# A gated attention stage with a shorter tile pipeline, GpSimd taking the scale and the add into X for six of eight groups, and another order of loads

## Time and profile before

| what | value |
|---|---|
| median of 3 runs | 2098.03 us |
| the 3 runs | 2091.5, 2098.03, 2098.66 us |
| the profiled execution | 2095.7 us, span 2093.8 us |
| PE busy over the span | 1423.5 us (68%) |
| DVE busy over the span | 1382.9 us (66%) |
| ACT busy over the span | 1120.2 us (54%) |
| POOL busy over the span | 498.2 us (24%) |

### The profile page before, as it was taken

The page is one execution under the profiler, slowest core; times in us unless marked ns, Lnnn a source line. Parts: engine busy times, 40 slices in busy tenths (PEclk is TensorE's granted clock), DMA queues, the critical chain, the costliest instruction groups (busy, mean ns, idle before and its releaser), DMA issues. The chain is left out here.

```text
span 2093.8 us, 33634 instructions
## 1 busy us (share of the span) xinstructions
PE 1423.5 (68%) x11186; PEld 871.1 (42%) x11186; DVE 1382.9 (66%) x2946; ACT 1120.2 (54%) x1552; POOL 498.2 (24%) x903
## 2 busy tenths in 40 slices
PE   3339999999569965988616666368998836675111
PEld 3315555555357742444411333235555522443010
DVE  6647878878244533587667999435565557874896
ACT  4517777777411213665527889523343426886454
POOL 4412233333310032111013343100101011211663
PEclk9999999999879986999855667679999958887555
DMA  5653555555310002333110000011101030000111
GB/s 168 203 123 76 127 128 128 134 127 133 69 46 0 0 5 40 67 66 67 37 64 1 0 1 0 26 31 27 36 24 37 12 106 1 1 1 9 42 50 41
DMA packets 100486, 118.01 MB, mean 56 GB/s; under 512 B 33825, under 2 KB 86249, under 8 KB 95757
## 3 DMA queue, kind: packets, MB, share of 16 engines
q1 hardware_dynamic: 100364, 116.48, 22.1%
HBM read 80.07 MB, written 22.88 MB: 49 GB/s over the span
## 5 line engine op out<-in xcount | busy, mean ns | idle before, releaser
L610 DVE TENSOR_REDUCE ratt_nmax<-ratt_psS 128x2 f32<-128x512 f32 x512 | 318.1, 683 | 95.7 <-PE ratt_psS L502 95.4
L576 ACT ACTIVATE ratt_E<-ratt_psT 128x1024 f32<-128x1024 f32 x256 | 255.0, 1023 | 108.7 <-PE ratt_psT L524 108.7
L502 PE MATMUL ratt_psS<-ratt_K,ratt_Q 72*128 72x256 bf16 x1024 | 204.1, 283 | 42.0 <-DMA ratt_K<-context_parts 36.8
L524 PE MATMUL ratt_psT<-ratt_Q,ratt_K 75*128 75x256 bf16 x1024 | 195.8, 275 | 4.9 <-DMA ratt_Q<-ratt_rows 4.6
L537 PE MATMUL ratt_psO<-ratt_E,ratt_V 128*32 128x256 f32 x2048 | 137.9, 387 | 0.7 <-ACT ratt_E L576 0.7
L502 PEld LDWEIGHTS ratt_psS<-ratt_K,ratt_Q 72*128 72x128 bf16 x1024 | 80.0, 99 | 138.2 <-issue 65.4
L524 PEld LDWEIGHTS ratt_psT<-ratt_Q,ratt_K 75*128 75x128 bf16 x1024 | 99.4, 98 | 22.7 <-DMA ratt_Q<-ratt_rows 5.0
L3388 PE MATMUL final_psT<-final_identh,final_Z 128*128 128x128 f16 x64 | 8.2, 310 | 110.7 <-ACT final_Z L3422 110.7
L1008 PE MATMUL gatt_psS<-heads_KX,gatt_QT 128*64 128x512 f32 x256 | 68.2, 657 | 12.2 <-DMA heads_KX<-all_CT 12.2
L2415 DVE TENSOR_REDUCE satt_mx<-satt_psS 128x16 f32<-128x1024 f32 x32 | 39.0, 1219 | 56.4 <-PE satt_psS L1008 56.4
L2190 PE MATMUL nffn_psH<-nffn_W,nffn_QT 128*128 128x512 bf16 x128 | 55.8, 585 | 29.1 <-ACT nffn_H L2269 20.3
(11 more groups left out here) (472 smaller groups left out, 3706.9 us busy)
## 6 DMA issues: line engine op xcount, KB each, us to landing
ratt_Q<-z_parts SPq DMA_DIRECT2D x32, 576.0 KB
ratt_K<-context_parts SPq DMA_DIRECT2D x96, 192.0 KB
gatt_V<-in_ctx_dram SPq DMA_DIRECT2D x16, 512.0 KB, 6.1
z_parts<-prep_ZS SPq DMA_DIRECT2D x48, 128.0 KB, 2.6
context_parts<-prep_CS SPq DMA_DIRECT2D x48, 128.0 KB, 2.3
head_sums<-ratt_O SPq DMA_DIRECT2D x64, 72.0 KB
all_X<-in_x_dram SPq DMA_DIRECT2D x8, 512.0 KB
prep_C<-in_ctx_dram SPq DMA_DIRECT2D x8, 512.0 KB
```

The costliest lines, as they stand in the source:

```text
L502: mm = nc.tensor.matmul(psS[:, RING[h], c * D:(c + 1) * D], Q9[0:R, buf, h, k % 2, c * P:(c + 1) * P], K9[0:R, buf, h, k % 2, :], start=Tr ...
L524: mm = nc.tensor.matmul(psT[:, p % 2, e, c, :], K9[0:RM, buf, h, u, c * P:(c + 1) * P], Q9[0:RM, buf, h, u, :], start=True, stop=True)
L576: nc.scalar.activation(E[:, 2 * b + p // 2, 2 * (p % 2):2 * (p % 2) + 2], psT[:, p % 2], ACT.Exp, scale=SCALE).then_inc(exped, 1)
L610: nc.vector.tensor_reduce(nmax[:, k % 2, h, :], psS[:, RING[h]].rearrange("p (c t) -> p c t", c=2), AX.X, ALU.max, negate=True).then_inc(m ...
```

```diff
@@ sync
                 for g in range(NG):
+                    if g > 0:
+                        sp.wait_ge(v_copied, g * 2)
+                        rows_of_context(g)
                     decay_rows(g)
                     if g > 0:
                         keys(g, 0)
-                        sp.wait_ge(v_copied, g * 2)
-                        rows_of_context(g)
                         keys(g, 1)
...
@@ gpsimd
+                def add(g):
+                    pool.wait_ge(s_steps, g * SPER + SPER)
+                    flat = cen[:, g % 2].rearrange("p j h d -> p j (h d)")
+                    gp.tensor_tensor(flat, flat, spread(lscale[:], 1, G), ALU.mult).then_inc(scaled, 1)
+                    pool.wait_ge(scaled, g + 1)
+                    xs = X[:, g * G:(g + 1) * G, :]
+                    gp.tensor_tensor(xs, xs, flat, ALU.add).then_inc(x_done, 1)
...
-                for g in range(NG):
+                for g in range(NG + 4):
                     if is_group(g + 1):
                         norm.on_pool(pool, g + 1)
-                    split_rows(g)
+                    if is_group(g):
+                        split_rows(g)
+                    if is_group(g - 4) and g - 4 < NG - 2:
+                        add(g - 4)
@@ vector
-                dve.wait_ge(ready, READY)
-                v.tensor_copy(R[:].rearrange("p w j c h t -> p (w j c) (h t)"),
...
                         if is_group(g):
                             running_maximum(g)
+                        if g == 0:
+                            dve.wait_ge(ready, READY)
+                            v.tensor_copy(R[:].rearrange("p w j c h t -> p (w j c) (h t)"),
...
-                        if is_tile(n - 7):
-                            weigh(n - 7)
+                        if is_tile(n - 5):
+                            weigh(n - 5)
...
@@ tensor
-                    t = n - 6
+                    t = n - 4
                     if is_tile(t):
                         decay(t)
                     if is_group(g) and g > 0 and i == 0:
                         turn_gates(g)
@@ scalar
                 def copy_gates(g):
                     act.wait_ge(gated, g + 1)
+                    if g > 0:
+                        act.wait_ge(split, g)
...
-                    if is_group(g - 1) and i == 3:
-                        place_values(g - 1)
```

More of the change, by code:

```diff
@@ L1065, in gated_attention @@
         gbias = s.sb("gbias", [NG2, 1])
-        GT = s.sb("GT", [NG2, G * P])
+        work = s.sb("work", [GH, G * P])
+        GT, rest = work[0:NG2], work[:].rearrange("p (n c t) -> p n c t", n=2, c=2)
         lscale = s.sb("lscale", [P, D])
@@ L1083, in gated_attention @@
         cen = s.sb("cen", [P, 2, G, NH, DH])
-        tw = s.sb("tw", [P, 11, G, NH])
+        tw = s.sb("tw", [P, 14, G, NH])
         psA = s.ps("psA", [P, 2, HC * L])
@@ L1097, in gated_attention @@
         ROWS_IN = 16 * 5
-        SLOTS = T + 15
+        SLOTS = T + 16
         def is_group(g):
@@ L1281, in tail_below @@
                     step(v.tensor_scalar(tw[:, 4], tw[:, 4], 1e-6, None, ALU.add))
-                    step(v.reciprocal(tw[:, 5], tw[:, 4]))
-                    step(v.tensor_tensor(tw[:, 8], tw[:, 5], tw[:, 5], ALU.mult))
+                    step(v.reciprocal(tw[:, 5 + 6 * (g % 2)], tw[:, 4]))
+                    step(v.tensor_tensor(tw[:, 8], tw[:, 5 + 6 * (g % 2)], tw[:, 5 + 6 * (g % 2)], ALU.mult))
                 def tail_variance(g):
@@ L1291, in tail_variance @@
                     step(v.tensor_scalar(tw[:, 1], tw[:, 10], 1.0 / DH, None, ALU.mult))
-                    step(v.tensor_scalar(tw[:, 6], tw[:, 1], 1e-6, None, ALU.add))
+                    step(v.tensor_scalar(tw[:, 6 + 6 * (g % 2)], tw[:, 1], 1e-6, None, ALU.add))
                     step.end()
@@ L1297, in tail_scale @@
                     dve.wait_ge(r_done, g + 1)
-                    step(v.tensor_tensor(tw[:, 4], tw[:, 7], tw[:, 7], ALU.mult))
-                    step(v.tensor_tensor(tw[:, 4], tw[:, 4], tw[:, 6], ALU.mult))
+                    step(v.tensor_tensor(tw[:, 4], tw[:, 7 + 6 * (g % 2)], tw[:, 7 + 6 * (g % 2)], ALU.mult))
+                    step(v.tensor_tensor(tw[:, 4], tw[:, 4], tw[:, 6 + 6 * (g % 2)], ALU.mult))
                     step(v.tensor_scalar(tw[:, 4], tw[:, 4], -0.5, 1.5, ALU.mult, ALU.add))
-                    step(v.tensor_tensor(tw[:, 9], tw[:, 4], tw[:, 7], ALU.mult))
-                    step(v.tensor_tensor(tw[:, 8], tw[:, 9], tw[:, 5], ALU.mult))
+                    step(v.tensor_tensor(tw[:, 9], tw[:, 4], tw[:, 7 + 6 * (g % 2)], ALU.mult))
+                    step(v.tensor_tensor(tw[:, 8], tw[:, 9], tw[:, 5 + 6 * (g % 2)], ALU.mult))
                     step(v.tensor_tensor(cen[:, g % 2], cen[:, g % 2], spread(tw[:, 8], 3, DH), ALU.mult))
                     step.end()
[L1305 to L1309, removed]
+                    if g >= NG - 2:
+                        flat = cen[:, g % 2].rearrange("p j h d -> p j (h d)")
+                        v.tensor_tensor(flat, flat, spread(lscale[:], 1, G), ALU.mult).then_inc(scaled, 1)
+                        dve.wait_ge(scaled, g + 1)
+                        xs = X[:, g * G:(g + 1) * G, :]
+                        v.tensor_tensor(xs, xs, flat, ALU.add).then_inc(x_done, 1)
                 norm.take_stats(dve, 0)
@@ L1325, in _ @@
                             front_gates(g)
-                        if is_tile(n - 7):
-                            weigh(n - 7)
+                        if is_tile(n - 5):
+                            weigh(n - 5)
+                        if is_group(g - 3):
+                            tail_below(g - 3)
                         if is_group(g):
@@ L1330, in _ @@
                         if is_group(g - 3):
-                            tail_centre(g - 3)
+                            tail_variance(g - 3)
                     if i == 1:
@@ L1340, in _ @@
                             running_maximum(g)
+                        if g == 0:
+                            dve.wait_ge(ready, READY)
+                            v.tensor_copy(R[:].rearrange("p w j c h t -> p (w j c) (h t)"),
+                                          spread(rbase[:].rearrange("p h t -> p (h t)"), 1, 2 * G * KC)).then_inc(const_set, 1)
+                            v.tensor_copy(LT[:].rearrange("p w j c u t -> p (w j c) (u t)"),
+                                          spread(lbase[:].rearrange("p u t -> p (u t)"), 1, 2 * G * KC)).then_inc(const_set, 1)
                     if i == 2:
-                        if is_tile(n - 7):
-                            weigh(n - 7)
+                        if is_tile(n - 5):
+                            weigh(n - 5)
                         if is_group(g):
@@ L1352, in _ @@
                     if i == 3:
[L1353 to L1358, removed]
+                        if is_tile(n - 5):
+                            weigh(n - 5)
+                        if is_group(g - 2):
+                            tail_centre(g - 2)
             @block.tensor
@@ L1501, in logarithms @@
                     if is_group(g - 4):
+                        odd = 6 * (g % 2)
                         act.wait_ge(v_steps, (g - 3) * VPER)
-                        sc.activation(tw[:, 10], tw[:, 6], ACT.Ln).then_inc(v_ln, 1)
+                        sc.activation(tw[:, 7 + odd], tw[:, 6 + odd], ACT.Ln).then_inc(v_ln, 1)
                         act.wait_ge(v_ln, g - 3)
-                        sc.activation(tw[:, 7], tw[:, 10], ACT.Exp, scale=-0.5).then_inc(r_done, 1)
+                        sc.activation(tw[:, 7 + odd], tw[:, 7 + odd], ACT.Exp, scale=-0.5).then_inc(r_done, 1)
                 def take_output(t):
@@ L1540, in _ @@
                         logarithms(g)
-                    if is_group(g - 3) and i == 1:
-                        tail(g - 3)
                     if is_tile(t - 2):
                         take_output(t - 2)
+                    if is_group(g) and i == 3:
+                        place_values(g)
                     if is_group(g + 1) and i == 3:
                         copy_gates(g + 1)
-                    if is_group(g - 1) and i == 3:
-                        place_values(g - 1)
+                    if is_group(g - 2) and i == 3:
+                        tail(g - 2)
 def ternary(nc, name, identb, matrices, loads=()):
```

5 lines of the change are left out of this document (1 added, 4 removed).

## The result

The changed kernel takes 2122.18 us (median of four runs, 2120.32 to 2128.55) beside 2095.3 (2091.5 to 2098.66) for the kernel before in the same comparison: ratio 1.0134, 95% interval 1.0104 to 1.0165. It is slower, by 27 us; 2100 was forecast, 2 us over the 2098.03 that three runs of the kernel before had given, with a range up to 2115. Its profiled execution has a span of 2120.0 us, 26.2 more than before. The stage's last addition ends at 1084.0, against 1062.0 in the earlier trace rows: 22.0 of the 26.2. The stage also starts 1.15 us earlier in this trace (its first load goes at 762.93, against 764.08), so it is itself 23.2 us longer. Of the other 4.2 us, 3.9 stand in the last layer, whose code is the same: from its load of the summaries to its first output it took 266.4 to 266.7 us in four of the thirteen traces here (the kernel before among them) and 269.1 to 271.3 in the others.

What follows compares the result with a forecast made beforehand. SP's queue of DMA issues was taken as the bound, at 28.1 us a group. Start +3.3, V2 out of the keys -1.4, end -1.0 and collisions +1 gave about +2 us on 2098.03: 2100, eight-in-ten range 2092 to 2115.

Steps and rivals of the forecast that it cites:

- The start: Stage start up to keys(1,0): decay rows of group 1 go 15.6 us later, at 831.9; keys(1,0) starts at 837.0, +3.3 us.
- second rival: SP's wait for the split at the decay rows: split comes behind SP in six groups, 2106 to 2118; chance 0.22.
- third rival: GpSimd's adds hold DVE off on the path: 2114, up to 2126; chance 0.06.
- The end: From SP's last issue to the last addition into X, 37.1 us before: forecast 1.0 us shorter.
- the 10.2 that were kept: From SP's last issue to the end of the last `weigh`: 10.2 us, assumed unchanged.
- the sum: Whole kernel: +3.3 - 1.4 - 1.0 + 1 = +1.9, called +2 us.
- -1.4 + 1: SP's queue after keys(1,0): 1.4 us less for the V2 no longer among the keys, 1 us more for collisions.
- the 1075: Sign at the stage's end: if it ends before 1055 or behind 1075, the prediction is wrong.
- fourth rival: SP's key blocks give way, so DVE and PE count: 14.7 us come back, 2085, faster; chance 0.07.

## Why the prediction was wrong

**Right.** SP's queue is the bound: merging its keys alone takes 24 us off the kernel before. **The start:** decay rows of group 1 were forecast at 831.9 and keys(1,0) at 837.0, and came at 830.52 and 835.50, 1.4 and 1.5 us early; 1.15 of that is the earlier start of the stage. Inside it two small errors offset each other: SP's first V2 goes 2.5 us sooner after the stage's first load than before, where 1.6 was forecast, and from the decay rows of group 0 to those of group 1 it is 23.9 us for 23.5. **The margin of the split** (second rival, 0.22) held: SP waited for a split at group 1 alone, here and with V2 between the halves. **The adds** (third rival, 0.06) don't show in the time of the kernel on either base. They do hold DVE off, as weighed: at the end of the stage a 128x64 instruction of DVE that takes 0.21 us alone took 2.13, to 1066.07, beside GpSimd's multiplication of group 5 (1063.65 to 1065.99).

```profile
1063.94 2.13 DVE L1281 TENSOR_TENSOR gatt_tw<-gatt_mx,gatt_cum 128x64 f32<-128x64 f32 x1 [0.37 <-ACT gatt_OG L1533]
...
1082.77 1.23 DVE L1324 TENSOR_TENSOR all_X<-all_X,gatt_cen 128x1024 f32<-128x1024 f32 x1
```

**The end:** from SP's last issue, 1026.63 + 20.95 = 1047.6, to 1084.0 it is 36.4 us; 37.1 - 1.0 = 36.1 was forecast. The parts are less right than their sum: behind the last `weigh`, which ends at 1057.1, it is 26.9 us, as long as before, where 25.9 was forecast, and the 0.7 us gained lie ahead of it (9.5 for the 10.2 that were kept).

**The step that failed** is in the paragraph on the start, and the sum carried it through all groups: "Behind the decay rows come the DRAM round trip, LT and R, in all 5.05 us". That price was read where V2 was 20 us away. For group 1 it held, since its V2 still stood 19 us ahead. For groups 2 to 7 the change put 1 MB right in front of the store, and the round trip grew by some 4 us each: from 5.05 to about 9.1 us (857.99 to 867.08 in group 2), and SP's wait for the store from 9.9 us in these six groups to 35.2 (37.0 with group 1). Of V2's move I counted only the 1.4 us that it took out of the keys, and took its transfer as hidden. No rival had it, and slower had a chance of 0.20 for other reasons. From keys(1,0) to the last issue SP needed 1047.6 - 835.5 = 212.1 us against 1024.9 - 833.6 = 191.3: +20.8, where -1.4 + 1 had been summed. With the start's +1.9 and the tail's -0.7 that is the stage's 22.0. Its end at 1084.0 also lies behind the 1075 that the prediction had named as the sign of being wrong.

The forecast of 2100 is nearly the time of the kernel with V2 between the halves (2099.33), which has every other part of the change: all other terms together were right to some 3 us (for the profiled execution 2097.7 was forecast, and that of V2 between the halves took 2100.94). The fourth rival (key blocks that give way) did not occur; blocks of 32 took 20.65 to 21.65.

**Where the gain went.** The rest of the change, the shorter pipeline above all, is worth 10.6 us, but only once SP doesn't bind.

## What to carry to other kernels

Where one queue issues everything and waits for one of its own small DMAs, look at what large transfer is in flight then, on whatever queue: the price of the round trip is that of its surroundings, and must be read again when the order changes. Put a large load where a long stretch of small issues (11 us were enough here, 4 were not) or another wait follows it, not ahead of a store that is waited for. If issuing is the bound, merge DMAs before touching the engines: halving the number of key loads brought 24 us to the kernel before, the whole change on top another 10.6, and moving vector work to GpSimd nothing.

## What the runs showed of the hardware

A 96 KB store to DRAM that took 2.4 us from its issue until SP went on took 6.0 to 7.4 when issued within some 2 us of 1 MB of loads: 6.4 to 7.3 behind them on the same queue, 6.0 to 7.4 with them on another. It took 3.1 to 4.7 behind 512 KB, and 3.7 to 4.5 when 3.9 to 4.5 us with six small DMAs had passed. Issued 0.1 us behind the loads it took about as long to land as they did (6.4 and 6.1 us median), though it has a tenth of their bytes. Whether the DMA engines or DRAM hold it up isn't shown. A DMA over 16 partitions costs SP's queue 0.63 to 0.69 us to issue with 16 KB, and 0.65 to 0.79 with 32 KB.
